# Attention bursts: the products for the row maxima move behind scores and value products, VectorE's passes over them behind the exponents

## The reference, cut to what matters

```python
scores = jnp.einsum('bhqd,bhkd->bhqk', q, k) * scale
scores = jnp.where(causal, scores, -jnp.inf)
attn = jax.nn.softmax(scores, axis=-1)
out = jnp.einsum('bhqk,bhkd->bhqd', attn, v)
geo = qp[..., :, None] * kp[..., None, :]
geo = jnp.where(causal, geo, -jnp.inf)
geo_attn = jax.nn.softmax(geo, axis=-1)
geo_out = jnp.einsum('bhqk,bhkd->bhqd', geo_attn, v)
out = out + head_scales[None, :, None, None] * jax.lax.stop_gradient(geo_out - out)
```

## Time and profile before

| | |
|---|---|
| runs | 2981.43 us median of 3 (2978.15 to 2981.79) |
| profiled execution | 2979.26 us, of which the profile's span is 2977.2 us |
| PE busy over the span | 2580.3 us (87%) |
| DVE busy | 2220.6 us (75%) |
| ACT busy | 1502.5 us (50%) |
| POOL busy | 560.2 us (19%) |
| attention phase, first scores to last exponential | about 296 to 1322 us of the span |

### The profile page before, as it was taken

One profiled execution on the slowest core, in us unless ns is written; L12 is line 12 of the kernel. 1 busy time (PEld: TensorE's weight loads), 2 busy tenths in 40 slices (PEclk: granted clock), 3 DMA queues, 4 the chain that ended last, 5 costly groups with the idle time before them and its releaser, 6 DMA issues. The chain is left out here.

```text
span 2977.2 us, 44176 instructions
## 1 busy us (share of the span) xinstructions
PE 2580.3 (87%) x14072; PEld 1549.8 (52%) x14072; DVE 2220.6 (75%) x4598; ACT 1502.5 (50%) x2807; POOL 560.2 (19%) x388
## 2 busy tenths in 40 slices
PE   4995999999899999974499999949979999995998
PEld 2442333333333333323377777638856777774777
DVE  4776888989898888957688888725547888883665
ACT  0230555555555555541366666614426666663433
POOL 0110000001010001015333333200003333330000
PEclk7996999999999999987799999979989999998999
DMA  2325343344444344317200000030001000001111
GB/s 84 113 100 151 84 132 102 101 123 107 117 136 120 101 113 113 86 55 248 66 9 9 9 9 9 2 120 17 20 17 48 9 9 9 9 6 36 55 61 39
DMA packets 123897, 204.83 MB, mean 69 GB/s; under 512 B 22560, under 2 KB 71008, under 8 KB 120400
## 3 DMA queue, kind: packets, MB, share of 16 engines
q1 hardware_dynamic: 109040, 163.96, 19.8%
q0 software_dynamic: 8832, 21.80, 2.4%
q10 hardware_dynamic: 5920, 17.75, 1.6%
HBM read 125.30 MB, written 54.26 MB: 60 GB/s over the span
## 5 line engine op out<-in xcount | busy, mean ns | idle before, releaser
L801 ACT ACTIVATE probs<-st_ps 128x1024 f32<-128x1024 f32 (+3 forms) x640 | 550.5, 894 | 468.3 <-PE st_ps L733 192.6
L749 PE MATMUL o_ps<-probs,vx 128*33 128x512 f32 (+3 forms) x2560 | 556.4, 558 | 0.0
L850 DVE SCALAR_TENSOR_TENSOR st_ps<-geo_rows,kp_t 128x512 f32<-128x512 f32 (+3 forms) x640 | 463.2, 742 | 60.9 <-ACT probs L801 58.0
L829 DVE TENSOR_REDUCE chunk_max<-a_ps 128x1 f32<-128x512 f32 (+3 forms) x640 | 361.1, 603 | 44.0 <-PE a_ps L718 24.1
L1224 PE MATMUL local_in_ps<-w_local,local_ht 128*128 128x512 f32 x1152 | 322.7, 417 | 9.8 <-ACT local_sq L1366 5.4
L1385 ACT ACTIVATE local_probs<-local_s_ps,local_bias,local_inv 128x256 f32<-128x256 f32 x512 | 283.0, 564 | 13.9 <-DVE local_bias L1480 13.9
L1660 PE MATMUL ff_ag_ps<-ff_ht_parts,w 128*128 128x512 f32 (+1 forms) x1056 | 259.8, 404 | 33.7 <-DVE ff_gate L1769 25.5
L718 PE MATMUL a_ps<-k,q 96*128 96x512 f32 (+3 forms) x640 | 237.6, 446 | 28.4 <-DVE chunk_max L829 22.2
L749 PEld LDWEIGHTS o_ps<-probs,vx 128*33 128x33 f32 x2560 | 126.7, 114 | 253.2 <-issue 219.8
L1392 ACT ACTIVATE local_pt<-local_pt_ps 128x512 f32<-128x512 f32 x256 | 152.4, 596 | 208.3 <-PE local_pt_ps L1282 200.3
L1476 DVE TENSOR_REDUCE local_top<-local_s_ps 128x4 f32<-128x1024 f32 x128 | 156.8, 1225 | 122.4 <-PE local_s_ps L1268 122.4
(11 more groups left out here) (170 smaller groups left out, 3698.2 us busy)
## 6 DMA issues: line engine op xcount, KB each, us to landing
geo_rows<-geo SPq DMA_DIRECT2D x64, 512.0 KB, 7.5
q<-q_parts SPq DMA_DIRECT2D x48, 256.0 KB, 4.2
k<-k_parts SPq DMA_DIRECT2D x48, 256.0 KB, 6.4
piece_lo<-in_pieces POOLq DMA_DIRECT2D x15, 768.0 KB, 5.5
weight_parts<-piece_hi SPq DMA_DIRECT2D x15, 768.0 KB, 3.3
weight_parts<-piece_lo SPq DMA_DIRECT2D x15, 768.0 KB, 5.9
raw<-out_t SPq DMA_DIRECT2D x128, 64.0 KB
shares_in<-shares SPq DMA_DIRECT2D x64, 128.0 KB, 4.8
```

The lines of the kernel that those rows point to most:

```text
L749: ins = pe.matmul(o_ps[kind * HALF:kind * HALF + VW, g % 2, off:GTOK], vx[s][:, j, :], probs[:, i % PSLOTS, kind, off:GTOK], start=j == 0, ...
L801: act.activation(probs[:, s % PSLOTS, :, off:GTOK], st_ps[:, s % 2, :, off:GTOK], ACT.Exp).then_inc(q["probs_ready"], 1)
L829: dve.reduce_max(chunk_max[:, it, c:c + 1], a_ps[:, n % 2, 0:width], AX.X).then_inc(q["a_used"], 1)
L850: ins = dve.scalar_tensor_tensor(out[:, off:GTOK], geo[:, 1, at], kp_t[:, j, ds(b, 1)].rearrange("p o -> p o"), geo[:, 0, at], ALU.add, AL ...
```

## The change

In PE's `turn` a burst before issued the products of its first two tiles, the two scores, the rows item if there is one, and the value products of the burst before. Now it issues scores, value products, and then all its items: two tiles, and the rows item behind them. In DVE's `turn` the reductions of a burst's tiles stood ahead of the exponents for the next burst; now they stand behind them. Nothing is added or removed.

```diff
@@ PE, turn
                         items = max_items(b, 2 * p) + max_items(b, 2 * p + 1)
-                        for item in items[:2]:
-                            maxima(*item)
                         scores(b, s, 2 * p)
                         scores(b, s, 2 * p + 1)
-                        for item in items[2:]:
-                            maxima(*item)
                         if p:
                             weigh(b, s, 2 * p - 2)
                             weigh(b, s, 2 * p - 1)
                         elif before:
                             weigh(b - 1, (s - 1) % SETS, NB - 2)
                             weigh(b - 1, (s - 1) % SETS, NB - 1)
+                        for item in items:
+                            maxima(*item)
@@ DVE, turn
                     for p in range(BURSTS):
-                        for i in (2 * p, 2 * p + 1):
-                            for item in max_items(b, i):
-                                maxima(*item)
+                        items = max_items(b, 2 * p) + max_items(b, 2 * p + 1)
                         for i in (2 * p + 2, 2 * p + 3):
                             if i < NB:
                                 exponents(b, i)
                             elif more:
                                 exponents(b + 1, i - NB)
+                        for item in items:
+                            maxima(*item)
                         if before and p == 11:
                             invert(b - 1)
                         if more and p >= LOW_AFTER:
```

## The result

The changed kernel takes 2987.1 us (median of 18 runs, 2981.7 to 2999.4), the kernel before 2979.5 us over as many (2977.5 to 2983.5, but for one execution of 4951.1 us, which the ratio leaves out). The ratio is 1.0026, interval 1.0020 to 1.0033: 7.6 us slower, where 33 were forecast. Slower was right, the size was not, though the measured time lies inside the range.

What follows compares the result with a forecast made beforehand. PE and DVE were both taken as nearly full, with PE standing at the rows items' transposes for DVE's reductions. Losses of 9 + 2 + 10 - 1 = 20 us plus 13 for the clock gave 2981.4 + 33 = 3014 us, range 2984 to 3056.

Steps and rivals of the forecast that it cites:

- the rows item as the costly move: At bursts 8, 14 and 0, scores no longer cover the transpose's wait and come later: losses of 9, 2 and 10 us.
- 9 + 2 + 10: Losses in us forecast for the rows items at burst 8, burst 14 and burst 0, in that order, without the clock.
- What the change does in an ordinary burst: nothing: In ordinary bursts both streams keep their places with tiles one burst late, so 320 bursts cost as before.
- Two terms taken as nothing: DVE's `invert` behind burst 11's reductions and `piece_low` ahead of exponents: each put at nothing, `invert` with 22 us gain as bound.
- 20 us without the clock: Whole forecast loss before clock falls: 9 at burst 8, 2 at burst 14, 10 at burst 0, less 1 once.
- The clock term: Longer stalls at bursts 8 and 14 lower PE's clock behind a quarter of 31: 8 falls of 1.7 us, 13 us.
- it falls already: At burst 0 the clock already fell behind the stall before the change, so no further falls were added there.
- The walks: Step-by-step timings of PE and DVE around the rows items, forecasting stalls of 1.4, 1.65 and 3.3 us at bursts 8, 14, 0.
- The one for burst 8: PE and DVE timed pass by pass: a stall of 1.4 instead of 0.69 us, 9 us over 16 such bursts.
- I took back 7 of the 8.9 us: Behind burst 14, a later PE waits less at the next tiles, cutting that burst's 9 us loss to 2.
- The clock falling at most of the longer stalls: Rival: low clock behind most of the longer stalls, 65 us or a little more, 3045 to 3060 us; chance 0.15.
- The stalls cancel: Rival: late rows items cost nothing where DVE and ACT set the path; 2976 to 2987 us; chance 0.14.
- GpSimd's products meeting reductions: Rival: at burst 16 later L670 spares exponents, 22 to 43 us gained, about 2960 to 2975 us; chance 0.09.

Runs made afterwards that it cites:

- e3: The changed kernel with PE's rows item back between the scores and the value products: 2970.7 us, ratio 0.9974 to the kernel before.
- e1: The kernel before with PE's half of the change alone, DVE keeping its old order: 3116.6 us, ratio 1.0459.
- e2: The kernel before with DVE's half of the change alone, PE keeping its old order: 3634.2 us, ratio 1.2196.
- e9: e3 with DVE's `invert` and `piece_low` both back between exponents and reductions: 2961.4 us, ratio 0.9933 to the kernel before.
- e6: e3 with only DVE's `piece_low` back between exponents and reductions: 2959.1 us, ratio 0.9923 to the kernel before.
- e7: e3 with ACT's and DVE's work on the weight piece 8 bursts earlier: 2930.6 us, ratio 0.9830 to the kernel before.
- e4: The kernel before with the rows item behind the value products on PE and behind the exponents on DVE: 2983.2 us, ratio 1.0013.

## Why the prediction was right or wrong

**Right: the sign, where PE stands, and the rows item as the costly move.** Putting the scores behind the transpose instead of between it and the tiles costs time. Forecast 21 us (9 + 2 + 10, without the clock), measured as e3 against the changed kernel 16 us, which is 26 us of waits less 11 of busy time that the clock gave back: so the nearness of 21 and 16 is in part luck. The time stays within the range 2984 to 3056, near its lower end, and the sign of the whole is luck in part too, since a term put at nothing was larger than this one and had the other sign.

**The step that failed first: "What the change does in an ordinary burst: nothing".** It was half right. The two streams are in step in both orders, and e1 and e2 show what it costs where they are not. But bursts differ in width, and a shift by one changes which meet where DVE is behind. The shift alone gives 20 us (e9), which the sum had at 0. The gain lies at burst 8, at burst 14 and behind it, and why it lies there is argued, not shown.

**Two terms taken as nothing were a loss.** `piece_low` was "three times a turn 0.68 us ... taken as nothing", with a gain of some tenths thought possible; `invert` had up to 22 us of gain as its bound. Both lose, together 12 us (e9 against e3, give or take 8). For the piece the rows show how: behind the reductions it lengthens the stall at burst 0 by 0.6 us (e6), of which the slot waits ahead of it take back half; the larger part of its gain in e6 is the clock. For `invert` they do not. So 20 us without the clock is in truth -20 + 12 + 16 = 8 us, and these are the measured terms with the clock in them. That they make up the 7.6 us is no test of them, since each is a difference between kernels of one chain. The traces of the chain split them; idle time is what the later end leaves when busy time is taken off:

| kernel | phase ends | PE busy, 296 to 1336 | idle against the row above | low level lost |
|---|---|---|---|---|
| before | 1323.3 us | 946.6 us | | 50.7 us |
| e9, shift alone | 1306.4 | 945.4 | -15.8 | 59.2 |
| e3, `invert` and piece behind | 1315.7 | 950.5 | +4.2 | 66.0 |
| changed, rows item behind | 1331.1 | 939.7 | +26.1 | 35.3 |

**The clock term had the wrong sign.** I added 13 us for falls behind stalls of 1.4 and 1.65 us. The stalls came out at 0.62 and 1.25, and behind these lengths the clock fell in neither kernel; it fell behind the one of 1.52 us, which each of the two traces of the changed kernel has in one turn. At burst 0, where I wrote "it falls already" and put nothing, the low level mostly lasted half as long. The two pairs of traces give 15 and 10 us of lost clock less than before. In PE's busy time that is 6.9 and 2.3 us, counted from the first transpose to the phase's end, in which both kernels have 4357 products.

**The walks.** The one for burst 8 erred by its gaps. The two pairs of exponents take 1.32 and 1.33 us from start to start where I had put 1.45 to 1.5, and the fold 0.48 where I had put 0.55; DVE was ahead of the walk by 0.5 us, and PE's products came 0.3 us later than written. Together this made 1.4 us out of 0.62. At burst 14 I took back 7 of the 8.9 us of slot waits behind it; 4.4 went. Two errors of a few tenths were a whole term, since a stall is a difference of two long sums. What stayed true is that the transpose follows the first tile's reduction.

**The rivals.** The clock falling at most of the longer stalls did not happen. "The stalls cancel" was nearest in time, but for the wrong reason: not a loss that is swallowed, but a gain and two losses beside it. GpSimd's products meeting reductions was seen in part. In the turn above both exponents fell under them, 4.19 us against 4.40. But in seven turns only one of the two passes did, as in the second row here, where before this was so in two:

```profile
804.42 4.19 DVE L848 SCALAR_TENSOR_TENSOR st_ps<-geo_rows,kp_t 128x512 f32<-128x512 f32 x2 [0.93 <-ACT probs L799]
...
1000.85 2.10 DVE L848 SCALAR_TENSOR_TENSOR st_ps<-geo_rows,kp_t 128x512 f32<-128x512 f32 x1 [0.67 <-ACT probs L799]
```

It paid little. DVE's passes that overlap L670 or L674, each less the median of the same pass elsewhere in the phase, sum to 33.6 us of delay in the changed kernel against 35.4 before (31.9 in e9, 24.5 in e3). That is 2 us of gain, where the rival wanted 22 to 43.

**Open.** Why the low clock at burst 0 lasts a shorter time in the changed kernel. The stalls are as long, so it is not their length; e3, with less idle time, lost 66.0 us to it, e9 59.2. What stands around the stall differs, and so does the length of a turn, and no run separates them. The traces narrow it: the stall is the same in every turn, but the moment at which the clock falls is not. In the first trace of the kernel before it fell between 1.1 us ahead of the transpose's start and 0.5 us behind it in the ten turns with the long stay, and 1.4 to 2.1 us behind it in the four with the short one. In the changed kernel's two traces it fell 0.8 to 2.2 us ahead in the five with the long stay, and between 0.2 us ahead and 1.4 us behind in the twenty-five others.

## What to carry to other kernels

Two engines that hand work to each other in a fixed order are in step or not, and that is the first thing to check of a move: here it is worth 137 or 655 us. Once they are in step, a shift by a whole burst is not nothing where the bursts differ in size: look at every stall of a turn, not at the longest alone, since the 20 us came from the shorter ones. And a stall that repeats every turn is best treated by moving work that nobody waits for away from it: the piece's passes on ACT and DVE, 8 bursts earlier, gave some 40 us (e7 against e3), two thirds of it through the clock, where moving the stalled instruction itself behind other work only moved the stall (e4).

## What the runs showed of the hardware

The granted clock answered to stalls of nearly the same length in different ways: 2.56 us before was followed by a low level (1.2 GHz) that lost 3.4 us in most turns, 2.62 after by one that lost 1.7 in most. A kernel with less idle time in the phase (e3, 64.6 us of waits) lost more to the clock (66.0 us) than one with 90.9 us of waits (35.3 us). Idle time alone does not give the price of the clock. Nor does one stall's length say whether the clock falls: of nine stalls of 1.32 or 1.33 us at burst 0 in e7, five were followed by the low level and four were not.
